# Conditional residual layers on one core: matrices formed before the cast of x and stored as halves, softmax first, and half of the output moves on ScalarE's queue

## The reference

```
x = x + L0(x); x = x + L1(x); x = x + L2(x); x = x + L3(x)
L0, L2:  h = gelu(gelu(c @ W0 + b0) @ W1 + b1); att = softmax(h @ W2 + b2)     # 8 weights per item
         out = (sum_k att_k * weight_k) @ x + att @ bias_k                      # one 128x128 matrix per item
L1, L3:  grouped convolution, 4 groups, 9 taps, along the points, + c_weight @ c + fside_S_0
```

## Time and profile before

| | us |
|---|---|
| median of 3 runs | 3067.23 |
| lowest, highest | 3064.52, 3067.24 |
| the profiled execution | 3059.13 |
| its span | 3057.3 |
| TensorE busy (share of the span) | 2919.7 (95%) |
| VectorE busy | 2050.8 (67%) |
| GpSimd busy | 1789.0 (59%) |
| ScalarE busy | 1458.8 (48%) |
| granted clock of TensorE, mean | 0.996 |
| busy share of the DMA engines, hardware queue | 60.8% |

### The profile page before, as it was taken

How to read it: one execution, slowest core, us unless ns; L and a number is a source line. 1 busy time by engine, 2 the same in 40 slices (tenths; PEclk the granted TensorE clock), 3 DMA queues, 4 the chain that set the end, 5 groups by cost and what they waited for, 6 DMA issues and landing times.

```text
span 3057.3 us, 123405 instructions
## 1 busy us (share of the span) xinstructions
PE 2919.7 (95%) x49220; PEld 2803.7 (92%) x49220; DVE 2050.8 (67%) x2587; ACT 1458.8 (48%) x2333; POOL 1789.0 (59%) x1801
## 2 busy tenths in 40 slices
PE   6999999999999999999999999999999999999998
PEld 5999999999999999999999999999999999998997
DVE  6666667666766666666666666766676666666664
ACT  4454444444454445444545444544444444544454
POOL 4565556565656565656556655665565656565653
PEclk8999999999999999999999999999999999999999
DMA  4665665566556666666666566666655665666554
GB/s 125 154 159 157 162 174 156 157 165 171 156 157 164 170 157 157 165 169 158 158 167 164 157 157 171 163 158 162 174 156 157 165 170 157 156 164 169 157 157 136
DMA packets 375112, 489.80 MB, mean 160 GB/s; under 512 B 63400, under 2 KB 227376, under 8 KB 358704
## 3 DMA queue, kind: packets, MB, share of 16 engines
q1 hardware_dynamic: 375088, 489.46, 60.8%
HBM read 205.04 MB, written 150.99 MB: 116 GB/s over the span
## 4 chain that ended last, share of the span: by engine, by line
SPq 47%; DMA 25%; DVE 16%; issue 7%; PE 3%; DVEq 1%; POOL 0%; ACT 0%; ACTq 0%
SPq L223 37%; DMA x_t<-x 24%; DVE m_sum L530 6%; SPq L178 5%; DVE prod L524 5%; DVE xp L490 5%; SPq L184 4%; PE ps L306 2%; PE ps L291 1%; SPq L221 1%; DMA m_raw<-mixed 0%; ACT x_t L456 0%; POOL xp L626 0%; DVEq L488 0%; DVEq L529 0%
## 5 line engine op out<-in xcount | busy, mean ns | idle before, releaser
L306 PE MATMUL ps<-y,conv_parts 32*128 32x512 f32 x36864 | 2743.1, 390 | 104.2 <-ACT o_ph L459 102.1
L306 PEld LDWEIGHTS ps<-y,conv_parts 32*128 32x128 f32 x36864 | 2495.4, 184 | 206.1 <-issue 154.1
L423 ACT ACTIVATE y<-ps,bias 128x512 fp32r<-128x512 f32 x1536 | 1011.5, 700 | 581.8 <-PE ps L306 548.6
L554 DVE SCALAR_TENSOR_TENSOR y<-ps,bias,y 128x512 fp32r<-128x512 f32 x1536 | 1075.4, 747 | 199.2 <-ACT y L423 195.5
L626 POOL TENSOR_TENSOR xp<-x_t,xp 128x512 fp32r<-128x512 f32 x512 | 788.7, 1573 | 9.3 <-DVE xp L490 9.3
L619 POOL TENSOR_TENSOR m_parts<-m_raw,m_parts 128x512 fp32r<-128x512 f32 x256 | 447.5, 1748 | 534.2 <-ACT m_parts L430 534.2
L490 DVE CAST xp<-x_t 128x512 fp32r<-128x512 f32 x512 | 185.5, 426 | 762.4 <-DMA x_t<-x 762.4
L291 PE MATMUL ps<-y,m_parts 32*128 32x512 f32 x6144 | 684.7, 396 | 0.0
L291 PE MATMUL ps<-xp,m_parts 32*128 32x512 f32 x6144 | 653.3, 391 | 7.3 <-issue 5.4
L430 ACT CAST m_parts<-m_raw 128x512 fp32r<-128x512 f32 x256 | 164.5, 643 | 973.3 <-DMA m_raw<-mixed 973.3
L291 PEld LDWEIGHTS ps<-xp,m_parts 32*128 32x128 f32 x6144 | 558.2, 184 | 16.3 <-issue 7.9
(11 more groups left out here) (40 smaller groups left out, 38.6 us busy)
## 6 DMA issues: line engine op xcount, KB each, us to landing
x_t<-x SPq DMA_DIRECT2D x512, 256.0 KB, 5.0
o_ch<-o_ph SPq DMA_DIRECT2D x2032, 64.0 KB, 2.0
out<-o_t SPq DMA_DIRECT2D x127, 1024.0 KB, 4.9
m_raw<-mixed SPq DMA_DIRECT2D x1024, 64.0 KB, 4.3
mixed<-m_sum SPq DMA_DIRECT2D x256, 64.0 KB, 1.6
conv_raw<-conv_w SPq DMA_DIRECT2D x2, 768.0 KB, 9.8
mix_sb<-mix_w SPq DMA_DIRECT2D x2, 576.0 KB, 9.8
out<-x_t SPq DMA_DIRECT2D x4, 256.0 KB, 4.5
```

The costliest lines, as they stand in the source:

```text
L306: ins = nc.tensor.matmul(ps[:, 4 + t, :], conv_parts[layer][rows, w, PH * q + p_in, :], src[rows, a, p_in, q:q + N], start=(k == 0), stop= ...
L423: nc.scalar.activation(dst, src, ACT.Identity, bias=bias[layer][:, k % WIDTH[layer]:k % WIDTH[layer] + 1]).then_inc(high_set[layer], 1)
L554: nc.vector.scalar_tensor_tensor(out=dst, in0=src, scalar=bias[layer][:, k % WIDTH[layer]:k % WIDTH[layer] + 1], in1=high.bitcast(fp32), o ...
```

## The change

VectorE makes the halves of a matrix itself, from the 128x128 sum: a copy to the high half and a subtraction, into a new buffer `m_own` (128 x 2 x 128). The store takes both halves (128 KB), the four loads bring both (128 KB each) straight into `m_parts`, whose axes change places (group, half, column); `m_raw`, ScalarE's `matrix_high` and GpSimd's `matrix_low` are gone. A load now waits until the mix of the item before has ended (`mm[layer]`), since it overwrites its matrix. On VectorE the matrices stand ahead of the cast of x (but for step 0). On SyncE the layer-2 load comes first in a step, for item i-1, and both stores stand ahead of the moves. SyncE issues the eight moves of banks 0 and 1; ScalarE issues the eight of banks 2 and 3 at the end of its step, behind a wait for the four `o_ph` copies and for `in_time` of the item before. In GpSimd's step 0 the low part of layer 3's weights comes after that of x. Ahead of the loop the softmax comes before the cast of x, and ScalarE copies its first attention table before it casts the convolution weights.

```
@@ -45,8 +45,8 @@
         m_sum = {l: sb(f"m_sum{l}", [128, C]) for l in MIXES}
-        m_raw = {l: sb(f"m_raw{l}", [128, G, C]) for l in MIXES}
-        m_parts = {l: sb(f"m_parts{l}", [128, 2, G, C], f32r) for l in MIXES}
+        m_own = {l: sb(f"m_own{l}", [128, 2, C], f32r) for l in MIXES}
+        m_parts = {l: sb(f"m_parts{l}", [128, G, 2, C], f32r) for l in MIXES}
         bias = [sb(f"bias{l}", [128, WIDTH[l]]) for l in range(NL)]
...
...
@@ -180,19 +180,20 @@
-                sp.wait_ge(summed[layer], j + 1)
-                sp.dma_start(scratch[layer // 2][bass.ds(j, 1)].rearrange("s c o -> (s c) o"), m_sum[layer][:]).then_inc(stored[layer], 16)
+                sp.wait_ge(own_set[layer], j + 1)
+                sp.dma_start(scratch[layer // 2][bass.ds(j, 1)].rearrange("s c w o -> (s c) (w o)"),
+                             flat(m_own[layer], "w o").bitcast(fp32)).then_inc(stored[layer], 16)
...
                 if not first and layer == 0:
-                    sp.wait_ge(m_set[layer], j)
+                    sp.wait_ge(mm[layer], 4 * j)
                 sp.wait_ge(stored[layer], 16 * (j + 1))
                 if not first and layer == 2:
-                    sp.wait_ge(m_set[layer], j)
+                    sp.wait_ge(mm[layer], 4 * j)
                 for q in range(G):
-                    sp.dma_start(m_raw[layer][CG * q:CG * (q + 1)],
-                                 scratch[layer // 2][bass.ds(j, 1)].rearrange("s (g c) o -> (s c) g o", g=G)).then_inc(m_in[layer], 16)
+                    sp.dma_start(m_parts[layer][CG * q:CG * (q + 1)].rearrange("c g w o -> c g (w o)").bitcast(fp32),
+                                 scratch[layer // 2][bass.ds(j, 1)].rearrange("s (g c) w o -> (s c) g (w o)", g=G)).then_inc(m_in[layer], 16)
@@ -207,22 +208,24 @@
             def step(i, inner):
+                if has(i, inner, 1) and (inner or i > 1):
+                    load_matrix(2, i - 1, False)
                 if has(i, inner, -1):
                     load_matrix(0, i + 1, not inner and i == -1)
-                if has(i, inner, 0):
-                    load_matrix(2, i, not inner and i == 0)
                 if has(i, inner, 3):
...
                     store_matrix(0, i + 2)
+                if has(i, inner, -1):
+                    store_matrix(2, i + 1)
+                if not inner and i == -1:
+                    load_matrix(2, 0, True)
                 if has(i, inner, 2) and (inner or not is_last(i)):
-                    for g in range(G):
+                    for g in range(G // 2):
                         sp.wait_ge(phases_set, nth(i - 2, g))
...
                             sp.dma_start(o_ch[CG * g:CG * (g + 1), p, :], o_ph[CG * p:CG * (p + 1), g, :]).then_inc(shuffled[p], 16)
-                if has(i, inner, -1):
-                    store_matrix(2, i + 1)
                 if has(i, inner, -2):
@@ -283,12 +286,12 @@
                 if t == 0 and k == 0:
-                    pe.wait_ge(m_set[layer], j + 1)
+                    pe.wait_ge(m_in[layer], 16 * G * (j + 1))
                 if t == 0 and n == 0:
...
                     wait_bank(t)
-                ins = nc.tensor.matmul(ps[:, t, :], m_parts[layer][rows, m, g, :], src[rows, a, g, :],
+                ins = nc.tensor.matmul(ps[:, t, :], m_parts[layer][rows, g, m, :], src[rows, a, g, :],
                                        start=(k == 0), stop=(k == MIX - 1))
@@ -398,11 +401,15 @@
-            conv_high_part(1)
-            for l in range(2):
+            def att_rows(l):
+
                 act.wait_ge(att_mm, 2 * l + 1)
...
                                ps[:, 6 - 2 * l, :].rearrange("c (k j) -> c k j", k=4)).then_inc(table_act, 1)
+
+            att_rows(0)
+            conv_high_part(1)
+            att_rows(1)
             for l in range(2):
@@ -422,12 +429,6 @@
                                      bias=bias[layer][:, k % WIDTH[layer]:k % WIDTH[layer] + 1]).then_inc(high_set[layer], 1)
-
-            def matrix_high(layer, j, first):
-                act.wait_ge(m_in[layer], 16 * G * (j + 1))
-                if not first:
-                    act.wait_ge(mm[layer], 4 * j)
-                nc.scalar.copy(m_parts[layer][:, HIGH], m_raw[layer][:]).then_inc(m_high_set[layer], 1)
@@ -437,8 +438,6 @@
                         high(0, i, q, segment(HIGH, q), by_phase(q), not inner and i == 0)
-                if has(i, inner, -1):
-                    matrix_high(0, i + 1, not inner and i == -1)
                 if before:
@@ -463,8 +462,13 @@
                         high(2, i - 1, p, y3[:, HIGH, p, 1:N + 1], ps[:, p, :], not inner and i == 1)
-                if now:
-                    matrix_high(2, i, not inner and i == 0)
+                if before and (inner or not is_last(i)):
+                    act.wait_ge(phases_set, 4 * (i - 1))
+                    if inner or i > 2:
+                        act.wait_ge(in_time_set, 4 * (i - 2))
+                    for g in range(G // 2, G):
+                        for p in range(PH):
+                            act.dma_start(o_ch[CG * g:CG * (g + 1), p, :], o_ph[CG * p:CG * (p + 1), g, :]).then_inc(shuffled[p], 16)
@@ -525,12 +529,16 @@
                 dve.wait_ge(scaled[layer], j + 1)
+                nc.vector.tensor_reduce(m_sum[layer][:], prod[layer][:], AX_X, ALU.add).then_inc(summed[layer], 1)
+                dve.wait_ge(summed[layer], j + 1)
                 if not first:
                     dve.wait_ge(stored[layer], 16 * j)
-                nc.vector.tensor_reduce(m_sum[layer][:], prod[layer][:], AX_X, ALU.add).then_inc(summed[layer], 1)
+                nc.vector.tensor_copy(m_own[layer][:, HIGH], m_sum[layer][:]).then_inc(own_high[layer], 1)
+                dve.wait_ge(own_high[layer], j + 1)
+                nc.vector.tensor_tensor(m_own[layer][:, LOW], m_sum[layer][:], m_own[layer][:, HIGH].bitcast(fp32),
+                                        ALU.subtract).then_inc(own_set[layer], 1)
             dve.wait_ge(first_in, 32)
-            x_high(0, True)
             for l in range(2):
@@ -540,6 +548,7 @@
                 nc.vector.tensor_scalar(att_sb[:, l, :], expo[:, l, :], inv[:, l:l + 1], None, ALU.mult).then_inc(att_set, 1)
+            x_high(0, True)
             conv_identity(1)
@@ -562,12 +571,14 @@
                         low(0, i, q, segment(LOW, q), by_phase(q), segment(HIGH, q))
-                if now and has(i, inner, -1):
+                if not inner and i == 0:
                     x_high(i + 1, False)
...
                     matrix(2, i + 1, not inner and i == -1)
+                if now and has(i, inner, -1) and (inner or i != 0):
+                    x_high(i + 1, False)
                 if not inner and is_last(i):
@@ -614,11 +625,6 @@
-            def matrix_low(layer, j):
-                pool.wait_ge(m_high_set[layer], j + 1)
-                nc.gpsimd.tensor_tensor(m_parts[layer][:, LOW], m_raw[layer][:], m_parts[layer][:, HIGH].bitcast(fp32),
-                                        ALU.subtract).then_inc(m_set[layer], 1)
-
             def x_low(j):
@@ -640,17 +646,13 @@
                     set_bias(0, i + 1)
-                if has(i, inner, -1):
-                    matrix_low(0, i + 1)
+                if now and has(i, inner, -1):
+                    x_low(i + 1)
                 if not inner and i == 0:
                     conv_low_part(3)
-                if now and has(i, inner, -1):
-                    x_low(i + 1)
                 if before and (inner or i - 1 < B):
...
                     set_bias(3, i - 1)
-                if now:
-                    matrix_low(2, i)
                 if before and (inner or not is_last(i)):
@@ -734,7 +736,7 @@
            for name, a in arrays.items()}
-    scratch = nc.dram_tensor("mixed", (2, B, C, C), mybir.dt.float32, kind="Internal").ap()
+    scratch = nc.dram_tensor("mixed", (2, B, C, 2, C), mybir.dt.float32, kind="Internal").ap()
     out = nc.dram_tensor("out", (B, C, T), mybir.dt.float32, kind="ExternalOutput").ap()
```

More of the change, by code:

```diff
@@ L115, in build_cond_resid @@
         summed = {l: sem(f"summed{l}") for l in MIXES}
+        own_high = {l: sem(f"own_high{l}") for l in MIXES}
+        own_set = {l: sem(f"own_set{l}") for l in MIXES}
         stored = {l: sem(f"stored{l}") for l in MIXES}
@@ L132, in build_cond_resid @@
         out_act, out_dve = sem("out_act"), sem("out_dve")
-        m_high_set = {l: sem(f"m_high_set{l}") for l in (0, 2)}
-        m_set = {l: sem(f"m_set{l}") for l in (0, 2)}
         bias_set = [sem(f"bias_set{l}") for l in range(NL)]
```

## The result

The changed kernel takes 2924.12 us (median of 4 runs, 2922.91 to 2925.01) against 3066.85 before: a ratio of 0.9536, 95% interval 0.9519 to 0.9552. The profiled execution took 2924.14 us, its span 2922.3. Run again beside other kernels it stood at 0.9544 (0.9531 to 0.9557).

The account below looks back on a forecast made before the run. Bound: SyncE's ring of moves, x load and VectorE work, which TensorE follows. Loop 138.3 us plus start 6 take the span from 3057.3 to 2913.0, the execution to 2914.8; with 3 added, 2918 us, range 2900 to 2995.

Parts of the forecast that it names:

- the loop's gain: 122 loop steps average 23.44 us against TensorE's own pace of 22.31; the 1.13 lost per step, 138.3 us in all, returns.
- Its ring: SyncE's round of moves, x load, VectorE's cast, product and reduce, then store: 23.32 us a step, which TensorE follows.
- The start: Before the loop, softmax ahead of x's cast brings the first mix0 forward; 6 us gained, range 3 to 9.
- The 3 us added for the median: Runs' median was 8.1 us above the profiled execution, partly jitter that goes; 3 us added to 2914.8 for 2918.
- ScalarE's issues: Eight moves issued at the end of ScalarE's step, 0.63 us each, 5.0 in all: hidden, barely.
- The cover of 0.84 us an issue: ScalarE's eight issues fit from 16.9 to 23.6 of a step; beyond 0.84 each, every 0.1 us costs 0.8 a step.
- Rival A: ScalarE's and SyncE's DMA queues wait for one another, ScalarE's issues become the bound: step 24.3, time 3159; chance 0.13.
- A pair: VectorE's new cast and subtract at 128x128 per matrix: between 0.37 and about 1 us, taken as 0.5.
- slack of 4: VectorE's low parts of y3 end at about 17.7 into the step and are due from 22.31 on.
- The slacks: x lands at 27.5, wanted at 35.5: 8 us; first o_ph copy ends near 12.1, due 13.96: 1.9.
- rival B: ScalarE's issues cost 0.85 to 0.97 us each; at 0.9 a step is 22.8 and the time 2978; chance 0.12.
- C: No change: another ring holds the pace near 23.4, only the start is gained, 3053, or the stall moves; chance 0.04.

## Why the prediction was right, and where it was not

**The bound and the size.** Right. The prediction put the loop's gain at 138.3 us (its 1.13 us a step is 1.134 unrounded; with 1.13 the product is 137.9), and the loop gave 137.9. Its ring (moves, x load, VectorE) is confirmed by two runs. Eight moves fewer in the kernel before took the whole loss away. The halves alone removed what held o_ph up and lengthened the ring by 4.2 us, and the mean step grew by 4.0.

**The start.** This term was mis-sized, in sign too: 6 us of gain were counted (3 to 9), 3.0 were lost. Mix0 did come forward, to 27.93 from 32.13, and softmax first made about 3 us of it. But I had followed only "step 2 would then wait for x_low" and not VectorE's step 0, where the cast waits for x and both matrices, one behind GpSimd's 3.5 us on the convolution weights, stand ahead of y2's low part. This is the whole miss: 2914.8 for the profiled execution against 2924.1, of which 9.0 are this term. Without the exception of step 0 the start gains 8.5 us (93.86 to 85.33), inside the 3 to 9 that were counted: the order in step 0 was what the term had left out. The 3 us added for the median had no counterpart, as the medians equal the profiled execution now.

**ScalarE's issues.** Right: 0.63 was taken, 0.614 is the median, and ScalarE was done before it must evict. The cover of 0.84 us an issue is 6.7 us in all, which 12 and 16 moves confirm (23.36 a step; 12 x 0.65 is 1.1 over). That the cover came out to the tenth is luck, since both of its ends were half a microsecond late. The issues begin 16.3 into the step and not at 16.9, as the first runs while the last eviction does (1005.66 against 1003.50 plus 2.79), and by the ring with 12 moves they must end near 23.1 and not 23.6, because of the 0.45 us behind the last. Rival A needed the two queues to wait for one another. They hardly do: where they overlap by 3.4 us a step the medians are 0.597 and 0.614, and in the run with 16 moves on ScalarE it is 0.612 for those that overlap no issue of SyncE. The lock on the descriptor generator, which the prediction drew from the Trainium skill, "Perfetto Trace Analysis", section "DMA Instruction — HWDGE (DVE, Sync)", can cost no more than some 0.015 us an issue by these medians. The other rule, from the Trainium skill, "DMA: Bandwidth & Descriptors", section "Issuing engines are not separate DMA queues", is that issuing from several engines at once only saves sequencer time, which "is usually small". What was saved here is sequencer time, but it was not small: 5 us of 23.4 a step in the ring that set the pace, and 0.9536 with that edit alone.

**What carried the gain.** The prediction said that most of the gain would be there without ScalarE's moves. The runs show both less and more: without them 73 of 141 us remain (2990 of 3063, where the whole is 2922), because of one late load; and with them alone everything is there. The change cuts the ring in two places. The new order on VectorE is enough alone once that load is in time (0.9537). ScalarE's moves are enough alone only on the kernel before (0.9536): beside the new halves and stores, with x cast first, they leave a ring of 24.9 us (1.0625).

**VectorE.** A pair costs what was said (0.23 + 0.29, against 0.5 with gaps). The casts of x did not: 3.63 instead of 1.44, beside GpSimd. The matrices end 14.1 into the step, within the 14.2 allowed, and the low parts of y3 end at 20.3 (1009.61), not near 17.7. Of the slack of 4 about 2 are left, which was enough.

**The slacks** of x (8 us) and o_ph (1.9) were not tried by themselves. No rival B or C showed in the changed kernel.

## What to carry to other kernels

When an engine's waits name a neighbour that itself waits for a load, follow the load's queue round to its own start: an ordered queue of DMA issues with engine work in it is a ring, and its length, added up from one round of the profile, is the step. Any cut that brings the ring below the bound engine's pace gives the whole gain and a second cut gives nothing, so test the parts one at a time; and a part that is enough alone may fail beside another part that lengthens the ring. In the queue, count to the landing and not to the issue, and look at the first steps, where an order that is right in the loop may cost several us once.

## What was not expected of the hardware

- Two queues issued DMAs at the same time and hardly slowed each other: medians 0.591 us on SyncE's queue (0.597 for the moves that overlap) and 0.614 on ScalarE's, 0.590 with one queue.
- A 128x512 cast took 0.36 us on VectorE alone and 0.97 (page mean 970 ns, 426 before) beside GpSimd's subtractions; a 128x128 copy of 0.23 took 3.24 behind one of 3.5 us.
- ScalarE took 0.45 us from the last DMA issue to its next eviction at the loop's end, with 12 moves and with 16.
- An idle time of 3.17 us was followed by a granted clock of 0.55 for about 3.8 us, which cost 1.5 us a step; one of 0.83 us was not. With halves alone the clock fell after 101 of TensorE's 124 waits at mix2, of 2.5 us and more, and not after 23 of 2.0 to 2.8 us.
